# Windowed attention in a transformer layer: products with the values of two steps in one lump

## The reference

```python
def _L0_attn_ref(x, w_qkv, w_proj):
    DIM, NHEAD, WINDOW = (256, 16, 128)
    ...
    attn = jnp.einsum('bhqd,bhkd->bhqk', q, k) / math.sqrt(DK)
    idx = jnp.arange(T)
    mask = jnp.abs(idx[None, :] - idx[:, None]) > WINDOW
    attn = jnp.where(mask[None, None], -1000000000.0, attn)
    p = jax.nn.softmax(attn, axis=-1)
    out = jnp.einsum('bhqk,bhkd->bhqd', p, v)
    out = out.transpose(0, 2, 1, 3).reshape(B, T, C)
    return jnp.einsum('btc,oc->bto', out, w_proj)
...
x = L0_attn_x
xn = _layernorm(x, axis=-1)
x = x + _L0_attn_ref(xn, ...) + _L0_ffn_ref(xn, ...)
```

## Time and profile before

| what | value |
|---|---|
| median of 3 runs | 1376.39 us (1376.28 to 1380.51) |
| span of the profiled execution | 1166.2 us |
| time of the profiled execution itself | not given by the page; 1376.39 - 1166.2 = 210.2 us lie around the span, by the median |
| attention, from the first score to the last turn of outputs | about 740 to 1126 us of the span |
| TensorE's granted clock over the span | 0.984 |

### The profile page before, as it was taken

One profiled execution on the slowest core, in us unless ns is written; L12 is line 12 of the kernel. 1 busy time (PEld: TensorE's weight loads), 2 busy tenths in 40 slices (PEclk: granted clock), 3 DMA queues, 4 the chain that ended last, 5 costly groups with the idle time before them and its releaser, 6 DMA issues. The chain is left out here.

```text
span 1166.2 us, 33945 instructions
## 1 busy us (share of the span) xinstructions
PE 1085.4 (93%) x8297; PEld 799.0 (69%) x8298; DVE 767.9 (66%) x2491; ACT 756.1 (65%) x1914; POOL 622.2 (53%) x658
## 2 busy tenths in 40 slices
PE   6989799599999999999999999699999999999999
PEld 3545456399999999999999999355545545455457
DVE  7777779734444444444444457589999998999933
ACT  2555367567777777777777776366666666666653
POOL 0444200176666666666666655466666666666620
PEclk9999899899999999999999999799999999999999
DMA  6888811278888888878877764366665576656413
GB/s 223 216 213 213 240 42 32 94 222 261 247 251 244 252 253 240 250 240 250 253 229 205 206 198 149 101 154 159 154 171 142 142 169 161 152 143 159 122 60 122
DMA packets 143000, 213.84 MB, mean 183 GB/s; under 512 B 19425, under 2 KB 115682, under 8 KB 142946
## 3 DMA queue, kind: packets, MB, share of 16 engines
q0 software_dynamic: 27648, 86.02, 27.6%
q1 hardware_dynamic: 70946, 84.42, 25.9%
q10 hardware_dynamic: 44352, 42.74, 10.6%
HBM read 142.59 MB, written 70.26 MB: 183 GB/s over the span
## 5 line engine op out<-in xcount | busy, mean ns | idle before, releaser
L1076 POOL DMA_INDIRECT xb<-token_rows,idx_ring_x x320 | 303.1, 947 | 179.2 <-issue 140.5
L1104 PE MATMUL psum<-xTe,wb_and_xT_all_or_onorm 128*128 128x128 f32 x2560 | 339.2, 276 | 0.0
L1724 POOL DMA_INDIRECT yg<-expert_rows,idx_ring x256 | 254.2, 993 | 122.5 <-PE psum L1452 45.3
L1227 DVE TENSOR_SCALAR ys<-psum,xb 128x256 f32<-128x256 f32 x320 | 154.9, 484 | 244.7 <-PE psum L1113 243.3
L1104 PEld LDWEIGHTS psum<-xTe,wb_and_xT_all_or_onorm 128*128 128x128 f32 x2560 | 312.4, 192 | 0.1
L1566 ACT ACTIVATE pT<-psum 128x384 f32<-128x384 f32 (+1 forms) x512 | 215.5, 467 | 135.6 <-PE psum L1452 127.7
L1626 DVE CUSTOM_DVE_ANT_0 masked<-psum,mask_q 128x384 f32<-128x384 f32 (+1 forms) x480 | 230.9, 518 | 20.6 <-PE psum L1459 17.2
L1177 ACT COPY wb_and_xT_all_or_onorm<-wb_and_xT_all_or_onorm 128x512 f32 x320 | 197.7, 619 | 18.5 <-SPq L1038 4.8
L1113 PE MATMUL psum<-wb_and_xT_all_or_onorm,aT 128*128 x640 | 191.8, 381 | 0.4 <-issue 0.2
L1163 ACT COPY xTe<-psum 128x256 f32<-128x256 f32 x320 | 119.1, 372 | 102.4 <-PE psum L1094 93.0
L1459 PE MATMUL psum<-qk 96*128 96x384 bf16 (+1 forms) x480 | 154.0, 321 | 29.7 <-DVE nmax L1626 18.4
(11 more groups left out here) (143 smaller groups left out, 1143.0 us busy)
## 6 DMA issues: line engine op xcount, KB each, us to landing
expert_rows<-ys ACTq DMA_DIRECT2D x160, 256.0 KB
wb_and_xT_all_or_onorm<-in_w_exp SPq DMA_DIRECT2D x64, 384.0 KB, 4.2
qk<-q_stacks SPq DMA_DIRECT2D x32, 384.0 KB
q_stacks<-wb_and_xT_all_or_onorm SPq DMA_DIRECT2D x32, 192.0 KB, 2.7
qk<-k_parts SPq DMA_DIRECT2D x32, 192.0 KB
k_parts<-wb_and_xT_all_or_onorm SPq DMA_DIRECT2D x28, 192.0 KB, 3.1
token_rows<-rows SPq DMA_DIRECT2D x8, 640.0 KB, 4.3
xb<-token_rows,idx_ring_x POOLq DMA_INDIRECT x320
```

The lines of the kernel that those rows point to most:

```text
L1076: nc.gpsimd.indirect_dma_start(out=xb[:, r, :], out_offset=None, in_=rows_d, in_offset=bass.IndirectOffsetOnAxis(ap=idx_ring[:, q, r:r + 1 ...
L1104: last = nc.tensor.matmul(banks[GU + r % NB][:, part * P:(part + 1) * P], wgu[:, r % NW, h, part * I:(part + 1) * I], xT[:, r % NX, h, :], ...
L1227: nc.vector.tensor_scalar(ys[:, r // 2 % YR, r % 2, :], banks[Y + r % 2][:, 0:D], xb[:, r % XR, bass.ds(e + W_COL, 1)], None, ALU.mult).th ...
L1724: nc.gpsimd.indirect_dma_start(out=yg[:, h, k, :], out_offset=None, in_=y_d, in_offset=bass.IndirectOffsetOnAxis(ap=idx_ring[:, h, k:k + 1 ...
```

## The change

The values of two steps are now done in one lump. After the scores of each even step j come the values of steps j - 2 and j - 1 (after step 0 those of steps 6 and 7 of the group before); after odd steps none. The lump has one wait at its head, for all exponentials of both its steps. `pT` holds the probabilities of four steps, and lies in the first part of `wb`, the buffer of the experts' weights, which is free by then. The first exponential of step j waits for the values of step j - 4. ScalarE copies the first half of the outputs in step 7 instead of step 6. The last lump of the program holds steps 6 and 7 of the last group.

```diff
--- before.py
+++ after.py
@@ -1308,7 +1308,10 @@
     mask_q, masked, nmax, nmax_b, nmaxT, nrow_in, s1_ready, s1_free, hi_done, nmax_ready, dve_tick, pe_tick = (
         opening[name] for name in ("mask_q", "masked", "nmax", "nmax_b", "nmaxT", "nrow_in", "s1_ready", "s1_free",
                                    "hi_done", "nmax_ready", "dve_tick", "pe_tick"))
-    pT = sb("pT", [P, 2 * HG, 3 * P])
+    LUMP = 2
+    NP = 2 * LUMP
+    pT = keep["wb"][:, 0:NP * HG * 3 * P].rearrange("p (n c) -> p n c", n=NP * HG)
+    assert NP * HG * 3 * P <= WARM * WCOLS and TT % NP == 0
     oT = sb("oT", [P, T])
     rec = sb("rec", [P, 2, HT, HG])
     idx_ring = sb("idx_ring", [P, 2, K], I32)
@@ -1479,7 +1482,7 @@
                 for hh in range(HG):
                     last = nc.tensor.matmul(
                         banks[OB + bank][32 * hh:32 * hh + 32, (a - HT * bank) * P:(b - HT * bank) * P],
-                        va[:, hh, j, :], pT[:, (j % 2) * HG + hh, (a - lo) * P:(b - lo) * P],
+                        va[:, hh, j, :], pT[:, (j % NP) * HG + hh, (a - lo) * P:(b - lo) * P],
                         start=(part == 0 and j == 0) or (part == 1 and j == 3),
                         stop=(part, j) in ((0, 4), (0, 7)), skip_group_check=True)
                 if b == hi:
@@ -1504,9 +1507,17 @@
                                                oT[:, (HT * half + t) * P:(HT * half + t + 1) * P], ident[:, :])
                 last.then_inc(s1_ready, 1)
 
+            def lump(g, first):
+
+
+                pe.wait_ge(p_ready, g * (HG * TT) + HG * (first + LUMP))
+                for j in range(first, first + LUMP):
+                    before_values(g, j)
+                    for part in range(2):
+                        values(j, part)
+
             def before_values(g, j):
 
-                pe.wait_ge(p_ready, g * (HG * TT) + HG * (j + 1))
                 if j == 0:
                     pe.wait_ge(va_ready, g * 2 + 1)
                     reach(pe, o_read, g * 2 - 1)
@@ -1530,16 +1541,14 @@
                     carry, qq = divmod(q + ahead[0], 2)
                     if i in (0, 3):
                         pe.wait_ge(qk_in[qq][i // 3], (b + carry) * (16 * LOADS) + 16 * LOADS)
-                before = (g, j - 1) if j > 0 else (g - 1, TT - 1)
-                exists = j > 0 or not is_first(g)
+                before = (g, j - LUMP) if j > 0 else (g - 1, TT - LUMP)
+                exists = j % LUMP == 0 and (j > 0 or not is_first(g))
                 for hh in range(HG):
                     scores_k(g, q, j, hh)
                     if ahead is not None:
                         scores_q(g, qq, i, hh)
                 if exists:
-                    before_values(*before)
-                    for part in range(2):
-                        values(before[1], part)
+                    lump(*before)
                 if j == TURN_AT[M_LATE]:
                     turn_maxima(g * 2 + 2, 1, g, M_LATE)
                 if j == TURN_AT[O_0] and not is_first(g):
@@ -1551,8 +1560,7 @@
 
             pe.wait_ge(va_const, 2)
             every(pe, group)
-            before_values(NG - 1, TT - 1)
-            values(TT - 1, 0)
+            lump(NG - 1, TT - LUMP)
             for half in range(2):
                 turn_outputs(NG * 2 - 1 + half, half, NG - 1, O_1 + 1 + half)
 
@@ -1561,9 +1569,9 @@
             def exponentials(g, j, hh):
                 lo, hi = window(j)
                 if hh == 0:
-                    reach(act, pv_done, g * TT + (j - 1))
+                    reach(act, pv_done, g * TT + (j - NP + 1))
                 act.wait_ge(s2_ready, g * (HG * TT) + (j * HG + hh + 1))
-                nc.scalar.activation(pT[:, (j % 2) * HG + hh, 0:(hi - lo) * P], key_bank(j, hh)[:, 0:(hi - lo) * P],
+                nc.scalar.activation(pT[:, (j % NP) * HG + hh, 0:(hi - lo) * P], key_bank(j, hh)[:, 0:(hi - lo) * P],
                                      ACT.Exp).then_inc(p_ready, 1)
 
             def copy_slots(i, h):
@@ -1598,7 +1606,7 @@
                             if j == 5 and not (isinstance(g, int) and g == NG - 1):
                                 act.wait_ge(pv_done, g * TT + HT)
                                 copy_values(g + 1, 0)
-                            if j == 6:
+                            if j == 7:
                                 copy_outputs(g, 0)
                     if j in (2, 6) and not is_last(g):
                         copy_slots(g + 1, j // 4)
```

## The result

The changed kernel takes 1372.48 us (median of 8 runs, 1368.76 to 1393.12), the kernel before 1378.72 us (8 runs, 1375.26 to 1387.68). The ratio is 0.9945, 95% interval 0.9924 to 0.9966: faster by 0.55%, about 7.6 us. It leaves out the one slow execution of the changed kernel (1393.12 us), and the two medians by themselves are 6.24 us apart. The forecast was +13.5 us, so its sign was wrong.

A forecast was written before the change was run, and what follows sets the result against it. VectorE was taken to set the pace in attention, not TensorE. Terms 8.9 + 9.0 - 5.7 + 1.3 = +13.5 us on 1376.4 gave 1389.9 us, slower by 1.0%, range 1381 to 1398 us.

The forecast's parts named there:

- what lies around it: Time outside the profiled span: 1376.39 - 1166.2 = 210.2 us, claimed to stay unchanged and added to the forecast span.
- Step 4 to 5: Lump of steps 2 and 3 behind step 4 delays step 5's first maximum: +0.59 us a group, +8.9 us in all.
- Step 0 to 1: Lump of steps 6 and 7 delays the turn of the maxima and their copy: +0.64 us a group, +9.0 us.
- Step 3 to 4: No values behind step 3, so the outputs' turn leaves earlier and the reciprocal stops waiting: -0.41 us a group, -5.7 us.
- Steps 2 to 3 and 6 to 7: Longer lumps behind steps 2 and 6 said to be covered by VectorE's work, margins 0.41 and 0.2 us: no cost.
- Rival D: Worse than forecast: lump seam costs 0.24 us (+6.7), or the margin behind step 6 is gone (+6); 1396 us, chance 0.10.
- Last group: Group without maxima, paced by ScalarE's exponentials; the final lump waits for all of step 7's: +1.3 us, between 0 and 2.5.
- Price of a lump: TensorE time: 0.64 us per added inner step, lumps 1.22 and about 1.43 us; each pair saves 0.24 us of TensorE.
- Four sets "at no cost": Four sets of probabilities instead of two, in another place, were claimed to cost nothing.
- A: TensorE is the bound and its saved 0.96 us a group is time: -14 us, 1362 us, chance 0.05.
- B: VectorE's work covers all lumps; only the gain behind step 3 is left: -5.7 us, 1370.7 us, chance 0.04.
- C: Only one of the two new waits appears: +4.5 us or less, 1377 to 1381 us, chance 0.08.

The follow-up runs named there:

- the pair (6,7) alone: Kernel before with only the values of steps 6 and 7 lumped, behind step 0 of the next group: 1383.15 us, ratio 1.0023.
- the two visits: Kernel before with each inner step's values split into two visits, 256 columns behind the second head, 128 behind the fourth: 1378.30 us, ratio 0.9985.
- neither pair alone: Kernel before with one lump only: steps 6 and 7 behind step 0, ratio 1.0023; or steps 2 and 3 behind step 4, ratio 1.0000.
- both together: Changed kernel with only two lumps, steps 6, 7 behind step 0 and 2, 3 behind step 4, copy in step 6: ratio 0.9920, again 0.9958.

## Why the prediction was wrong

**The step that failed is the base**: "what lies around it (1376.39 - 1166.2 = 210.2, from the median of three runs, since the page gives no own time) stays". About 2 us lie around a span (1378.73 against 1376.8, 1379.72 against 1377.8). The 210 us were pauses inside the experts and attention of the timed runs. Every walk from row to row, with margins of 0.1 to 0.6 us, was made in an execution that has none, and was then added to a time in which a group takes 29.9 us, not 23.87. What this did to the terms: the two waits forecast in full came out at about half in the mean, emptying step 7, which the forecast puts at nothing, won 1.21 us a group, and the two covered lumps cost 0.58 and 0.75.

**What bounds.** "VectorE sets the pace" rested on 92.28 us of 100. In the timed kind of run it is 70% busy in attention and stands 88 us at its maxima. Covers and margins worked out from its being full do not hold there.

**Step 4 to 5, +0.59.** Measured 3.79 to 4.12, +0.33. The lump is there, between the score that it delays and the split that ended long before. The changed kernel, end of a step 4, TensorE and VectorE, to be laid beside the earlier trace rows:

```profile
1144.10 1.51 PE L1483 MATMUL psum<-wb_and_xT_all_or_onorm,va 128*32 128x256 f32 x32
1145.99 0.32 PE L1470 MATMUL psum<-qk 98*128 98x384 bf16 x1 [0.38 <-issue]
...
1146.75 0.32 PE L1462 MATMUL psum<-qk 96*128 96x384 bf16 x1 [0.32 <-issue]
...
1145.56 0.18 DVE L1647 TENSOR_TENSOR nmax_b<-nmax,nmax_b 128x20 bf16<-128x20 f32 x1
1147.49 0.56 DVE L1634 CUSTOM_DVE_ANT_0 masked<-psum,mask_q 128x384 f32<-128x384 f32 x1 [1.76 <-PE psum L1462]
```

VectorE waits 1.76 us here, as foretold in kind (0.6 to 0.7 was the size). But this wait holds a pause as well as the lump: behind the lump TensorE itself idles 0.38 and 0.32 us for nothing that the trace shows. And the kernel before already stretched this step by 3.79 - 2.53 = 1.26 us. That the lump's 0.64 went half into that stretch is one reading of the mean; it is argued, not shown, and the same lump costs this step +0.70 when it stands alone.

**Step 0 to 1, +0.64.** Measured 3.51 to 3.87, +0.36, where 1.37 us of stretch stood before. This is a mean of two heaps, one below the 3.75 to 3.79 us of before and one above (given with the table), and with the pair (6,7) alone the same lump costs +1.10. So here too "half of it" is no rule. A group of the upper heap, 1161.48 - 1157.16 = 4.32 us, lump, turn and copy, TensorE and VectorE of the changed kernel, beside the earlier trace rows:

```profile
1157.86 2.36 PE L1483 MATMUL psum<-wb_and_xT_all_or_onorm,va 128*32 128x256 f32 x24
1159.98 0.31 PE L1497 MATMUL psum<-consts_bf,nmax_b 128*24 128x128 bf16 x1
...
1157.16 0.42 DVE L1634 CUSTOM_DVE_ANT_0 masked<-psum,mask_q 128x256 f32<-128x256 f32 x1 [0.55 <-issue]
...
1159.82 0.42 DVE L1634 CUSTOM_DVE_ANT_0 masked<-psum,mask_q 128x256 f32<-128x256 f32 x1 [1.49 <-remote]
...
1160.43 0.21 DVE L1653 COPY nmaxT<-psum 24x128 bf16<-24x128 bf16 x1 [0.17 <-issue]
1161.48 0.56 DVE L1634 CUSTOM_DVE_ANT_0 masked<-psum,mask_q 128x384 f32<-128x384 f32 x1 [0.84 <-issue]
```

The idling before the copy and x(1,0) is 0.17 + 0.84 = 1.01 us, the 1.0 that was forecast. That is luck: the last maximum of the step waited 1.49 us just before, and the lump ran at the lower clock (below), neither of which was in the walk.

**Step 3 to 4, -0.41.** Right as a walk. In 26 of 39 groups the step takes 2.64 to 2.66 us, against 3.11 in the first profile, -0.47. The turn leaves early and the reciprocal follows the maximum with no wait, where the earlier trace rows had one (changed kernel, TensorE, then VectorE):

```profile
1022.73 0.66 PE L1506 MATMUL psum<-ident,oT 128*128 128x128 f32 x4
...
1023.07 0.55 DVE L1634 CUSTOM_DVE_ANT_0 masked<-psum,mask_q 128x384 f32<-128x384 f32 x1
...
1023.55 0.25 DVE L1660 RECIPROCAL rec<-psum 128x16 f32<-128x16 f32 x1
1023.95 0.42 DVE L1663 TENSOR_TENSOR wb_and_xT_all_or_onorm<-psum,rec 128x256 f32 x1
```

The mean gain is larger, 3.60 to 2.89, -0.71, since most of the step's pauses went with its values.

**Step 7 to 0.** Not in the prediction at all, and the largest term: 3.79 to 2.58, -1.21. Without pauses the step took 2.43 us and there was nothing to win. Steps 1 and 5 give -0.16 and -0.19 in the same way.

**Steps 2 to 3 and 6 to 7, "covered".** Measured 4.45 to 5.03 (+0.58) and 3.79 to 4.54 (+0.75): the margins of 0.41 and 0.2 us were those of a full VectorE. The first did hold in 6 of 39 groups, where step 2 takes 3.93 us as in the first profile (3.94); step 6 takes 3.79 us or more in all 39, against 3.22. Rival D named the second. The sum a group is +0.36 - 0.16 + 0.58 - 0.71 + 0.33 - 0.19 + 0.75 - 1.21 = -0.25 us, 13 groups -3.3, where +0.82 was forecast. The groups fell, which the prediction gave as a sign of being wrong. Losses of the four lengthened steps are +2.02, the gains of the four emptied ones -2.27. The difference of these two is the group's effect, and it is smaller than the spread between two profiles of one kernel (385.9 and 390.7 us for 13 groups); that the change gains rests on the timed ratios, not on this table. The first group (-2.3 us), group 14 (-1.8) and the tail (+1.6) are of the same size.

**Last group, +1.3.** Within its bounds: the tail, from the last maximum to the end, went from 64.8 to 66.4, +1.6 us (two profiles of before differ by 1.3, and the first profile has 59.9, so pauses are in it as well). Its mechanism is in the timeline of the changed kernel, TensorE and ScalarE, beside the earlier trace rows: the copy stands between the exponentials, and the lump waits for the last of them.

```profile
1326.01 0.59 ACT L1596 COPY oT<-psum 128x512 f32<-128x512 f32 x1
1326.47 0.69 ACT L1574 ACTIVATE wb_and_xT_all_or_onorm<-psum 128x256 f32<-128x256 f32 x2
...
1327.22 1.29 PE L1483 MATMUL psum<-wb_and_xT_all_or_onorm,va 128*32 128x256 f32 x24 [0.97 <-ACT wb_and_xT_all_or_onorm L1574]
1328.44 1.43 PE L1506 MATMUL psum<-ident,oT 128*128 128x128 f32 x8
```

**Price of a lump.** Right at the high clock: 1328.44 - 1327.22 = 1.22 us, and two inner steps 1153.35 - 1151.90 = 1.45 (1.43 forecast):

```profile
1151.90 1.51 PE L1483 MATMUL psum<-wb_and_xT_all_or_onorm,va 128*32 128x128 f32 x32
1153.35 0.28 PE L1470 MATMUL psum<-qk 98*128 98x256 bf16 x1
```

Wrong where the clock is down. The lump of step 0 takes 1159.98 - 1157.86 = 2.12 us, and the windows view (the clock is the third number from the right) has 0.51 there, the lower of the two levels (1.2 GHz), against 1.00 at the one above. In the stretch ahead of it TensorE was busy 1.83 us of 2.80:

```profile
1151.90:1153.40 1.50, 1.50 (x34) 0.95 (x34) 1.50 (x7) 0.52 (x2) 1.18 (x2) 1.00 0.44 128
1157.86:1159.98 2.12, 2.12 (x25) 1.19 (x25) 0.64 (x5) 0.38 (x1) 0.73 (x1) 0.51 1.09 285
...
1155.00:1157.80 2.80, 1.83 (x15) 1.08 (x15) 2.19 (x13) 2.15 (x7) 2.05 (x3) 1.00 0.31 52
```

The granted clock of all attention is 0.98 in the first profile, 0.95 in the next one of before and 0.92 after the change, so some of what the lumps win may go back here; no run separates it.

**Four sets "at no cost".** Shown on the chip without pauses (1.0002, and 1.0006 with the copy in step 7); on another, with the copy in step 7, it measured 1.0033.

**Rivals.** A (TensorE bound, 1362 us) falls with the two visits. The Trainium skill (TensorEngine Tiling (Array Packing), Key Properties) says that changing the tiling mode drains TensorE. The traces agree that going in and out costs TensorE something, 0.24 us, and paying six more of that a group changed nothing. B's time (1370.7) is nearest to the measured 1372.48, but not its mechanism: lumps are not covered, four of them cost +0.33 to +0.75 each. C and D gave times above the measured one.

**What is shown and what stays open.** Shown: pauses in executions of before and after alike whose time is that of the timed runs; where values leave a step nearly all of its pauses leave; neither pair alone measured a gain, both together did; it is not TensorE's time at the entries, and not the number of instructions. Not shown: how the change gains; the table puts the largest gain at step 7, but (6,7) alone wins as much there and loses it elsewhere. Open: what makes the pauses, why they sit with the values of some steps and not of others, and why both pairs are needed. All runs compared within a batch are from one chip, so whatever differs between chips is in both sides of a ratio; no run tried what that is. Open too is the sign on a chip without pauses. There the forecast's walk stands as it was, +13.5 us on 1168, and no run of the changed kernel was made on such a chip; of its terms only the -0.41 (as -0.47), the lump's price and the four sets were seen. In float32 I know of no version that beats the changed kernel by more than the intervals: two lumps gave 0.9920 and 0.9958, four gave 0.9941 to 0.9949.

## What to carry to other kernels

Lay the profile's span beside the timed runs before anything else: if they differ by more than the 2 us around it, the profile is of another kind of execution, and neither its busy shares nor its margins are those of the time you forecast. Where a step is already stretched by waits that the walk does not explain, a longer absence of an engine cost anything from half to nearly twice what the walk says (+0.36 and +1.10 us for one and the same lump, 0.64 by the walk), a margin of less than half a microsecond mostly covered nothing, and emptying a step may win the stretch that stood in it. And a gain of one part need not be a part of the gain: two halves that measured +0.2% and 0.0% gave -0.4 to -0.8% together.

## What the runs showed of the hardware

One program, with the same work, took 1168 us on one chip and 1378 to 1381 us (medians of batches) on five others. The first 230 us were equal and the experts and attention 22 and 25% longer. The extra time shows as late starts: VectorE and ScalarE start 1.7 to 1.8 us after the end of what they wait for on TensorE; from the start of a product to the start of its maximum the first profile has 0.55 us and the stretched one 2.15. Single instructions take nearly the same time (VectorE in attention 339 us busy against 336), and so do DMA packets. Such executions also recorded fewer changes of semaphores for the same program, 14400 to 15200 against 23800. In them 640 more idle instructions cost about 4.3 us, 7 ns each, and 1024 more products with their weight loads about 17 us, 17 ns a pair. Entering and leaving the values' 32-column products costs TensorE 0.24 us. A lump of the same rows took 1.22 us at the upper level of TensorE's clock (2.4 GHz) and 2.12 us at a granted 0.51, after a stretch of 2.80 us in which TensorE was busy 1.83.
